# Tokens turned by VectorE and DRAM instead of TensorE, four more products in parts, and a new order of the steps

## The reference

```python
xn = _layernorm(x)                                   # x: 8 x 512 x 256, float32
qkv = xn @ qkv_w + qkv_b                             # 256 x 768
attn = softmax(einsum('bnhd,bmhd->bhnm', q, k) * D ** -0.5)   # D = 16
out = einsum('bhnm,bmhd->bnhd', attn, v).reshape(b, n, c) @ proj_w + proj_b
gate, up = xn @ (w_gate / 127).T, xn @ (w_up / 127).T         # integer weights, 768 x 256
return x + out + (silu(gate) * up) @ (w_down / 127).T
```

## Time and profile before

| | |
|---|---|
| median of 3 runs | 602.68 us (602.6 to 602.72) |
| the profiled execution | 603.45 us |
| its span, first to last instruction | 601.7 us, mean granted clock 0.991 |
| busy: PE, DVE, ACT, POOL | 96%, 75%, 70%, 48% |
| DMA traffic | 59.18 MB, mean 98 GB/s |

### The profile page before, as it was taken

One profiled execution on the slowest core, in us unless ns is written; L12 is line 12 of the kernel. 1 busy time (PEld: TensorE's weight loads), 2 busy tenths in 40 slices (PEclk: granted clock), 3 DMA queues, 4 the chain that ended last, 5 costly groups with the idle time before them and its releaser, 6 DMA issues.

```text
span 601.7 us, 13743 instructions
## 1 busy us (share of the span) xinstructions
PE 575.6 (96%) x4844; PEld 338.6 (56%) x4844; DVE 453.8 (75%) x575; ACT 418.5 (70%) x572; POOL 286.2 (48%) x271
## 2 busy tenths in 40 slices
PE   8879999999999999999999999999999999998896
PEld 7646446555656556555665547555565557554453
DVE  5975767888777886788777886787778877788742
ACT  3555866888667866788668875778758876687563
POOL 3273426744565625754366444755267445253120
PEclk9989989999999999999999999999999999999999
DMA  8780145122842137221761129221561219320101
GB/s 280 231 146 9 36 142 151 47 55 89 194 124 55 53 115 183 52 53 53 196 155 36 53 85 230 53 53 53 158 159 35 54 54 216 103 55 20 54 2 37
DMA packets 38608, 59.18 MB, mean 98 GB/s; under 512 B 6320, under 2 KB 21680, under 8 KB 38576
## 3 DMA queue, kind: packets, MB, share of 16 engines
q1 hardware_dynamic: 38576, 58.75, 36.7%
HBM read 37.23 MB, written 20.97 MB: 97 GB/s over the span
## 4 chain that ended last, share of the span: by engine, by line
PE 84%; DVE 8%; ACT 3%; issue 2%; POOL 2%; DMA 1%; DVEq 0%; SPq 0%; ACTq 0%; POOLq 0%
PE dense L1180 29%; PE o_bank L1154 18%; PE st_bank L1121 14%; PE s_bank L1138 11%; PE dense L1209 6%; DVE neg_max L905 5%; PE dense L1164 2%; PE dense L1272 1%; ACT probs L757 1%; PE dense L1280 1%; POOL xn L660 1%; DMA xn<-in_L_attn_x 0%; DVE stats L887 0%; POOL rstd L654 0%; PE dense L1261 0%
## 5 line engine op out<-in xcount | busy, mean ns | idle before, releaser
L905 DVE TENSOR_REDUCE neg_max<-s_bank 128x2 f32<-128x1024 f32 x250 | 305.3, 1221 | 77.7 <-PE s_bank L1138 75.7
L757 ACT ACTIVATE probs<-st_bank 128x1024 f32<-128x1024 f32 x250 | 256.8, 1027 | 110.3 <-PE st_bank L1121 107.5
L1154 PE MATMUL o_bank<-probs,v_ones 128*32 128x512 f32 x1024 | 136.9, 607 | 0.0
L1121 PE MATMUL st_bank<-q_stack,k_stack 50*128 50x512 f32 x500 | 118.2, 468 | 5.6 <-ACT probs L757 5.0
L1138 PE MATMUL s_bank<-k_stack,q_stack 48*128 48x512 f32 x500 | 107.3, 423 | 3.5 <-DVE neg_max L905 2.5
L1121 PEld LDWEIGHTS st_bank<-q_stack,k_stack 50*128 50x128 f32 x500 | 47.2, 184 | 110.7 <-ACT probs L757 68.3
L669 POOL TENSOR_TENSOR gated<-gated,hid 128x512 f32<-128x512 f32 x48 | 61.7, 1286 | 46.1 <-DVE gated L927 31.3
L675 POOL TENSOR_TENSOR hid_tl<-gated,hid_th 128x512 fp32r<-128x512 f32 x48 | 61.7, 1285 | 38.4 <-ACT hid_th L851 38.4
L1138 PEld LDWEIGHTS s_bank<-k_stack,q_stack 48*128 48x128 f32 x500 | 47.6, 185 | 26.2 <-DVE neg_max L905 19.7
L1180 PE MATMUL dense<-xn_tl,w_gh 64*128 64x512 f32 x176 | 62.0, 392 | 0.0
L1180 PE MATMUL dense<-xn_tl,w_uh 64*128 64x512 f32 x176 | 61.9, 391 | 0.0
(11 more groups left out here) (155 smaller groups left out, 844.7 us busy)
## 6 DMA issues: line engine op xcount, KB each, us to landing
q_spread<-qk_parts SPq DMA_DIRECT2D x16, 512.0 KB, 3.7
k_spread<-qk_parts SPq DMA_DIRECT2D x16, 512.0 KB, 3.5
q_stack<-q_spread SPq DMA_DIRECT2D x64, 128.0 KB, 3.0
k_stack<-k_spread SPq DMA_DIRECT2D x64, 128.0 KB, 3.2
q_stack<-q_spread SPq DMA_DIRECT2D x64, 64.0 KB, 3.2
...
```

The costliest lines, as they stand in the source:

```text
L757: nc.scalar.activation(probs[:, s % 2, 2 * half:2 * half + 2, :], transposed_bank(row, s, half)[:, :, :], ACT.Exp, scale=SCALE).then_inc(e ...
L905: nc.vector.tensor_reduce(neg_max[:, g % 2, :, NT * pair + qt], score_bank(row, half)[:, :, :], AX_X, ALU.max, negate=True).then_inc(max_d ...
L1121: done = nc.tensor.matmul(transposed_bank(row, s, half)[:, r, :], k_stack[rows, pair, P * kt:P * (kt + 1)], q_stack[rows, pair, :], start= ...
L1154: done = nc.tensor.matmul(o_bank[32 * j:32 * (j + 1), :], v_ones[:, kt, 8 * (g // 2) + 2 * j + g % 2, :], probs[:, (s - 1) % 2, j, :], sta ...
```

## The change

1. **Tokens.** x is loaded in four DMAs so that the token tiles are interleaved over the partitions (`x_blocks`). GpSimd writes the normalised tokens into `xn_blocks`, 32 channels to a block. Two VectorE transposes of 32x32 blocks (`turn_blocks`, at `TURN_AT`, steps 12 and 13 of the row before) put them back into `xn`; SP stores them to a DRAM tensor `x_turned` in four DMAs, waits until these are done and loads them back as `xn_wide`. ScalarE splits them from there (`TOKENS_SPLIT_AT`, steps 2 and 3). The eight TensorE transposes and two ScalarE copies of each following row go.
2. **Products.** proj, q 1 and k 1 are made in parts as well. Their adds, and those of v, q 0 and k 0, stand in slot 2, behind the second maxima of their step. One part of proj goes over ScalarE into `p_part` and is added on GpSimd (`add_projection`).
3. **Steps.** `STEADY` is laid anew: every step has a product. proj moves from steps 4 and 7 to 2 and 3; up and gate 4 move from step 0 to step 14 of the row before.
4. **Maxima.** The chunk "max" stands ahead of P @ V and not behind it.
5. **Delays.** `INVERT`, `DIVIDE`, `RETURN`, `HIGH`, `LOW` are shorter by one slot each. The copies q and k in DRAM hold three parts, so that a stack is loaded by 4 DMAs and not 8, and the high part is stored before the low part is made.
6. **Row -1.** The three sums of squares that decide whether the weights are exact stand one by one; normalising row 1's tokens moves from step 7 to step 13; up and gate 4 are made here too.

```diff
-SPREADS = 2
-STACK_LOADS = 8
+SPREADS = 4
+STACK_LOADS = 4
 STEADY = [
-    (0, 0, "up", 4, 0, (2,)), (0, 0, "gate", 4, 0, (0,)),
-    (1, 0, "v", 1, 0, (1, 2)),
-    (2, 0, "up", 5, 0, (1,)), (2, 0, "gate", 5, 0, (0,)), (2, 1, "max", 1, 0, (2,)),
-    (3, 0, "xn", 0, 1, (1,)), (3, 0, "xn", 1, 1, (2,)),
-    (4, 0, "proj", 0, -1, (0, 1)),
+    (0, 0, "up", 5, 0, (0,)), (0, 0, "gate", 5, 0, (1,)),
+    (1, 0, "v", 1, 0, (2, 0)),
+    (2, 0, "proj", 0, -1, (2, 1)), (2, 0, "max", 1, 0, (0,)),
+    (3, 0, "proj", 1, -1, (0, 2)),
+    (4, 0, "q", 0, 1, (1, 0)),
...
-IN_PARTS = (("v", 0), ("v", 1), ("q", 0), ("k", 0))
+IN_PARTS = tuple((kind, i) for kind in ("v", "q", "k", "proj") for i in range(2))
-SQUARES_AFTER = ("gate", 1)
-DECISION_AFTER = ("max", 0)
-STATS_AT = ((5, 1), (6, 1), (7, 1), (10, 1))
-AVERAGE_AT = (10, 2)
-RESID_AT = ((8, 0), (9, 2))
+SQUARES_AFTER = (("wdown", 2), ("k", 1), ("max", 0))
+DECISION_AFTER = ("v", 0)
+STATS_AT = ((4, 1), (5, 1), (6, 1), (7, 1))
+AVERAGE_AT = (7, 2)
+RESID_AT = ((7, 0), (7, 1))
-ROW1_AVERAGE_AT = (7, 2)
+ROW1_AVERAGE_AT = (13, 2)
+TURN_AT = ((12, 1), (13, 1))
+ROW1_TURN_AT = ((0, 1), (0, 2))
+TOKENS_SPLIT_AT = ((2, 2), (3, 1))
-LEAVE, INVERT, DIVIDE, RETURN, HIGH, LOW = 1, 2, 2, 4, 5, 5
+LEAVE, INVERT, DIVIDE, RETURN, HIGH, LOW = 1, 1, 1, 3, 4, 4
...
+            def turn(at):
+                sp.wait_ge(turn_done, KC * at)
+                places = x_turned.rearrange("(b r) (q n) -> q r b n", r=32, q=NT)
+                for q in range(NT):
+                    sp.dma_start(places[q], xn[32 * q:32 * (q + 1), :, :]...).then_inc(turned_out, 16)
+                sp.wait_ge(turned_out, 16 * NT * at)
+                sp.dma_start(xn_wide, x_turned.rearrange("(k p) n -> p k n", p=P)).then_inc(turned_in, 16)
...
+            def add_projection(row, chunk):
+                pool.wait_ge(act_free, count(row, freed_by_act, chunk))
+                pool.wait_ge(dve_free, count(row, freed_by_dve, chunk))
+                nc.gpsimd.tensor_tensor(both, p_part[:, i, :]..., both, ALU.add).then_inc(projected, 1)
...
+            def turn_blocks(half, number):
+                dve.wait_ge(xn_done, NT * (number + 1))
+                nc.vector.transpose(xn[:, 2 * half:2 * half + 2, :]..., xn_blocks[:, n * half:n * (half + 1), :, :]...)
...
+                    if (kind, i, h) == ("proj", 0, 0) and (a, b) == (0, 0):
+                        pe.wait_ge(ot_low0, row.at)
+                        pe.wait_ge(ot_high, 2 * row.at - 1 + k)
+                    if (kind, i, h) == ("proj", 0, 0) and (a, b, k) == (1, 0, 1):
+                        pe.wait_ge(ot_low1, row.at)
```

281 lines of the change are left out of this document (163 added, 118 removed), and 13 rows, old and new, of tables (FIRST_IN_ORDER, STEADY).

## The result

The changed kernel takes 611.54 us, the median of 4 runs (609.8 to 613.62), against 602.7 us for the kernel before (4 runs, 602.6 to 605.91): a ratio of 1.0141, 95% interval 1.0111 to 1.0171. The forecast was 600.7, its range 588 to 609: the time lies outside it, and on the other side. 611.5 is nearly the 612 of rival R2, but not by R2's mechanism, as will be seen.

What follows compares the result with a forecast made beforehand. TensorE's in-order queue was taken as the bound (PE busy 68.60 of a steady row's 69.10 us). Terms -2.0 - 1.8 + 1.5 - 0.5 + 0.8 summed to -2.0, giving 600.7 us, range 588 to 609.

Steps and rivals of the forecast that it cites:

- R2: Rival: the chain scores, maxima, scores binds in every light step, 11 us more, 612 us; chance 0.14.
- row -1: Stretch before row 0: an old wait and half clock partly won back, -2.0 us, bounds -5 and +1.
- (d): Steps 12 and 13: block transposes cost 0.1 us, earlier maxima about -0.1, trip through DRAM nothing; 0 in all.
- row 0: First row, without projection: 67.5 us against 69.34, -1.8, with 0.6 included for a lowered clock.
- unhindered row: Steady row by TensorE's work alone, without (a) to (d): 66.6 us, 2.5 less than 69.05.
- (a): Projection ahead of step 2's transposed scores: waits for the last group's low part, +2.0 us a row, bounds 1.0 and 3.0.
- (b): Step 4: statistics, transpose and reciprocal on VectorE between its two maxima, +0.4 us a row, bounds 0 and 0.6.
- (c): Steps 7 to 9: GpSimd's normalising before division makes the second exponential late, +0.4 us a row, bounds 0 and 1.5.
- steady row's total: Rows 1 to 5: 66.6 + 2.0 + 0.4 + 0.4 = 69.4 us, 0.3 more than before.
- light steps: Steps whose product is of v's size: 3.80 us each, 3.7 to 4.0 expected if the forecast is right.
- R4: Rival: trip through DRAM late, q 0 waits, by GpSimd's late normalising; +1 us a row, 607 us; chance 0.05.
- R3: Rival: the wait of (a) lowers TensorE's clock in each row, 12 us more, 613 us; chance 0.07.

Runs made afterwards that it cites:

- e16_max0: e12_norm with SyncE's loads of the last group's and the next row's first maxima moved earlier, block transposes at (13, 1) and (14, 1): 585.95 us, ratio 0.9706.
- e7_stats: e4_cut_turn with the first of the four statistics on VectorE moved from step 4 to the start of step 5: 604.02 us, one execution.
- e14_delays: The changed kernel with only the delays set back to those of the kernel before (1, 2, 2, 4, 5, 5): 616.45 us, one execution.
- e12_norm: Changed kernel with projection at steps 3 and 6, banks given out anew, old delays, row 1's tokens early, normalising at step 10: 596.88 us, ratio 0.9903.
- e13_short: e12_norm with the changed kernel's shorter delays (1, 1, 1, 3, 4, 4): 606.14 us, ratio 1.006.
- e1_average: The changed kernel with GpSimd normalising row 1's tokens in row -1 behind step 6 instead of step 13: 612.83 us, ratio 1.0139.
- e2_turn: e1_average with row 1's tokens also turned in steps 11 and 12 of row -1: 609.96 us, ratio 1.0119.
- e4_cut_turn: e2_turn with five, not ten, terms of the projection's first product ahead of the next transposed scores: 602.05 us, ratio 0.999.
- e8_later: e4_cut_turn with the steady rows' normalising on GpSimd moved from step 7 to step 8: 601.52 us, one execution.

## Why the prediction was wrong, step by step

Two terms of the sum failed: row -1, put at -2.0 us and measured at +2.1, and in (d) the trip's cost of nothing, with the clock's fall that row 0 was priced for at 0.6 us; row 0 came out at +3.4 against -1.8. They are 4.1 and 5.2 of the 11.2 us between forecast and profile, and the fall of the clock in row 2 is 1.5 more. One by one:

- **The unhindered row, 66.6 us.** Right as a sum: e16_max0 has a row of 66.9 once little stands in its way, 2.2 us under the kernel before. How much of this each part (transposes, adds, products in parts) gives, no run shows.
- **(a), the projection's wait, +2.0 a row.** Right in chain and place, too large by 0.5. The step also transposes maxima, so that the forecast for it is 3.80 + 2.0 + 0.21 = 6.01 us, and it took 5.48 to 5.50. The waits are 1.14 us of that, and the exponential behind ScalarE's high part would hold the step at 5.05 without the low part's wait.
- **(b), +0.4.** The size is right (4.14 against 3.72), but its working has a slip: 0.41 + 0.72 + 0.23 is 1.36 and not 1.2, which would have given 0.6. The reason is right only in part: the statistics are 0.10 of it (e7_stats), the delays about 0.25 (e14_delays).
- **(c), +0.4.** Size right (4.95 against 4.23 + 0.21), reason incomplete: in the changed kernel this step takes 4.87 even where nothing is normalised, and 4.42 there with the old delays (e14_delays).
- **The steady row's total, 69.4 against 69.5, was in part luck.** In row 3 (a) is 0.5 less than forecast and the five other light steps are 0.4 less together. Against this v 1's step is 0.2 longer than a light step, the two down steps 0.3 together and five up steps 0.4 together, none of which was in the sum; (c) is 0.1 more.
- **What (a) to (c) lack** is one mechanism: a shorter delay puts an instruction that waits ahead of an exponential or a reduction in an ordered queue. It is 1.3 to 2.1 us a row where the projection has time (e12_norm against e13_short). I had seen it for VectorE's maxima in (a), and for ScalarE named it only in (c).
- **(d), the trip costs nothing.** Right for steady rows: no wait for x_turned there. Wrong in row 0, where it starts two steps ahead and not four. The wait is the smaller part of row 0's loss: 1.2 us where the clock held (e14_delays), and 1.0 to 1.5 by the rows with a fall (72.77 with the wait, 71.29 and 71.73 all but without it). The larger part, 3.5 us, is the fall of the clock. That the wait caused it is not shown: e1_average and e2_turn had the fall all but without the wait, e14_delays the wait without a fall. Row 0 with neither takes 67.4 to 67.8 us (e4_cut_turn, e8_later), where the forecast had 66.9 and 0.6 for a fall; that its sum of 67.5 lies so near is chance. R4 had the trip's wait for every row and for another reason, GpSimd's late normalising.
- **Row -1, -2.0.** Wrong by 4.1 us in the profiled execution (0.8 of it scatter at the very start), with row 0 starting at 52.70 us and not at 47 to 50. It was the least worked out term: a third of a bound, not a sum. The won wait and half clock were there (1.00 up to row 0). Not in the forecast at all was the wait for the first key stack, 2.48 us here and 1.8 to 3.0 in e1_average to e4_cut_turn and e14_delays; in e1_average and e4_cut_turn the clock fell behind it as well (0.64 and 0.76 from 28 to 32 us). Its stack is loaded from the copies in DRAM that the change laid out anew, but no run tests what makes it late. Up and gate 4, which came in, were named and never priced: PE's timeline has 1.6 us for each of the two, 3.2 in all, though row 7 gives a product back. Normalising early gave 0.7 (e1_average). The bare branch, 0.90 us of waiting, is no loss: the kernel before waits 0.78 at the same place. Neither the stack nor the two products were tried one by one, so the split of the rest stays open.
- **The clock, R3 at 0.07.** Underrated and drawn too uniformly: I priced it as seven falls in seven rows or none. Real falls come in a row now and then, 1.5 us behind the projection's wait, 3.5 us in row 0.
- **R2**, whose time of 612 us was all but measured, fell: most light steps take 3.71 to 3.73 us, within the forecast's 3.7 to 4.0, and PE waits for `neg_max` only 4.1 us in the whole program. That its number fits is chance.
